# The head of a conditional residual kernel: adapter rows loaded ahead of the ids, adapters in falling order, and the work of the head in another order on every engine

## The chip, the cores and the metric

One core of a Trainium2 chip runs the kernel. The metric is the device time of one launch in microseconds (us), lower is better. Engines: TensorE (PE) multiplies, VectorE (DVE), ScalarE (ACT) and GpSimd (POOL) work on elements, SyncE (SP) here only issues DMAs; ACT issues DMAs too.

## The reference, cut to what matters

```python
# x: (128, 64, 1024) f32; cond ids in 0..15, adapter ids in 3..7, one of each per sample
# L0 weights: (16, 64, 64); L1 weights: (8, 1024, 1024)
x = x + einsum('bct,bcd->bdt', x, L0_weights[cond_ids])
x = x + einsum('bsi,boi->bso', x, L1_weight[adapter_ids])
```

With a one added on the diagonal of both weights each step is a single product. The ids of these inputs give 19, 27, 23, 25 and 34 samples to adapters 3, 4, 5, 6 and 7.

## The kernel before

The 128 samples are sorted by adapter on the chip and dealt into slots of two samples with one adapter: 66 slots, of which the last of an adapter with an odd count holds one sample. For a slot PE first makes z = x times the adapter (1024 x 1024, in two halves n of 512 columns, KT = 8 row tiles), then y = z times the 64 x 64 condition weight. Products are kept exact by splitting every operand into a high part and the rest: `sum_z` does three products a tile (L557, L558, L560), and only two (no L560) where the slot holds one sample, whose rest then stands in the rows of the missing sample. `sum_y` (L570) is four products. PE's order of work in slot s: first half of z of s, y of slot s - 1, second half of z of s. The last slot has an order of its own (`sum_last_z`, L638 to L641, in pieces of 512, 256 and 256 columns, `sum_last_y`, L652), with DVE and ACT taking y out of the banks (L786, L1086) and stores by SP (L498, three, or two with one sample) and ACT (L810, one, none with one sample).

Who does what for a slot: SP loads x of slot s + 2 (eight DMAs, L442) and one chunk of 128 rows of the next adapter (four DMAs, L459), if there is one to load: the first eight slots after the first of each adapter load one each. POOL adds the one to the chunk (L305) and makes the low part of x (`xt_lo`, L353) and of the chunk (L370). DVE turns the chunk (L975), makes the low part of z's first half (L998), finishes y of the slot before (L1005), turns x of slot s + 2 (L990), and makes the low part of z's second half (L998), in that order. ACT makes the high parts (L699, L704, L695), spreads the condition weights (L709), moves y (L715) and stores y (L263). Every engine runs its own list in order and waits on semaphores.

The head, before the first product (L557), is straight code:

- SP loads the adapter ids as one row, the condition weights (w0, L400), waits for `first_known`, reads the smallest adapter id and loads its first two chunks (L409), waits for `samples_made`, loads x of slot 0 (L420) and the other six chunks; chunks 6 and 7 go into the places of chunks 0 and 1 and wait until those are turned. Then the table of slots is moved into one row (L424), and x of slots 1 and 2 is loaded from `table_i` (L442). Then it waits for the last turning and for `table_ready` (L1048), and the loop of slots begins.
- ACT loads both kinds of ids once more, one to a partition (L675, L676).
- DVE clips the ids in a row (L852 to L859) and in a column (L862 to L870), builds `member` (L871), finds the two samples of slot 0 (to L887), and from the counts of members (`counted`, PE L524 and L525) ranks the samples (L890 to L918, `hot_made`); PE gathers by rank (L599, L600), and DVE makes the table (L923 to L947, `table_made`). `link` makes each op wait for the one before.
- For each chunk POOL adds the one (L312), PE turns it (`turn_first`, eight transposes, L538) into a pair of banks of which there are three, ACT copies the high part (L687) and DVE makes the low part (L831) in two halves n. x of slot 0 is turned in the same row of steps (`TURN_ORDER`); the last chunk's turning stands behind the first nine products. A turning waits until the low part three steps before is made.
- w0 gets its one from POOL (L339), its high part from ACT (L750), its low part from POOL (L345).

## Time and profile before

| what | us |
|---|---|
| median of 3 runs | 795.91 |
| range of these runs | 795.88 to 796.24 |
| the profiled execution | 799.4 |
| its span, first to last instruction | 797.7 |
| busy in the span: PE, DVE, ACT, POOL | 780.7, 590.1, 455.9, 254.5 |

The page of the profile gives busy time by engine, the chain of work that ended last, and the costliest groups of instructions. The trace behind it can be asked for the instructions of one stretch in order of time, for waits, and for busy time by stretch. Times in the rows are microseconds from the start of the span, unless a column says otherwise.

### The profile page before, as it was taken

How to read it: one execution, taken by the hardware profiler on the slowest of the kernel's cores; microseconds unless marked ns; L12 is line 12 of the kernel's file. 1: busy time of each engine (PE TensorE's matmuls, PEld its weight loads, DVE VectorE, ACT ScalarE, POOL GpSimd, SP SyncE). 2: the span in 40 equal slices, each digit the busy share in tenths (PEclk: the TensorE clock that was granted, in tenths of full speed). 3: DMA queues.
4: the chain of work that ended last, by engine and by line, in shares of the span. 5: the costliest groups of instructions: out<-in, count | busy, mean ns of one | idle time of the engine just before them, and what ended most of it. 6: DMA issues, size and time to landing. Idle time of an engine off the chain costs nothing.

```text
span 797.7 us, 19299 instructions
## 1 busy us (share of the span) xinstructions
PE 780.7 (98%) x3480; PEld 646.8 (81%) x3481; DVE 590.1 (74%) x707; ACT 455.9 (57%) x773; POOL 254.5 (32%) x158
## 2 busy tenths in 40 slices
PE   5999999999999999999999999999999999999997
PEld 4788888888888888888888888888888888888885
DVE  7777987788887567888876788887576756756764
ACT  3565666566556555765655566566554654555554
POOL 1444434243452212335431243452122122122110
PEclk9999999999999999999999999999999999999998
DMA  8345454444532334444333444532332233233133
GB/s 249 98 110 153 128 144 122 124 123 138 154 99 85 105 91 119 128 148 139 98 105 105 121 121 141 156 97 88 105 96 76 78 105 91 67 105 102 60 102 81
DMA packets 73956, 90.91 MB, mean 114 GB/s; under 512 B 13781, under 2 KB 64470, under 8 KB 73942
## 3 DMA queue, kind: packets, MB, share of 16 engines
q1 hardware_dynamic: 63654, 58.11, 24.2%
q10 hardware_dynamic: 10288, 32.65, 14.4%
q8 instruction: 5, 0.08, 0.0%
q14 instruction: 9, 0.07, 0.0%
HBM read 57.15 MB, written 33.55 MB: 114 GB/s over the span
## 4 chain that ended last, share of the span: by engine, by line
PE 97%; DMA 2%; DVE 0%; POOL 0%; issue 0%; SPq 0%; ACT 0%; POOLq 0%
PE z_ps L557 15%; PE z_ps L558 15%; PE first_ps L557 15%; PE first_ps L558 15%; PE z_ps L560 15%; PE first_ps L560 13%; PE y_ps L570 7%; DMA w_nat<-in_L_cond_weight_dram 2%; PE y_ps L538 0%; PE first_ps L538 0%; PE first_ps L641 0%; PE first_ps L639 0%; PE first_ps L638 0%; PE y_ps L652 0%; POOL w_nat L312 0%
## 5 line engine op out<-in xcount | busy, mean ns | idle before, releaser
L353 POOL TENSOR_TENSOR xt_lo<-x_turned,xt_hi 128x1024 fp32r<-128x1024 f32 x61 | 146.6, 2403 | 250.5 <-ACT xt_hi L699 246.5
L557 PE MATMUL z_ps<-w_hi,xt_hi 128*128 (+1 forms) x528 | 205.8, 390 | 0.0
L558 PE MATMUL z_ps<-w_lo,xt_hi 128*128 (+1 forms) x528 | 205.4, 389 | 0.0
L557 PE MATMUL first_ps<-w_hi,xt_hi 128*128 x520 | 202.4, 389 | 0.0
L558 PE MATMUL first_ps<-w_lo,xt_hi 128*128 x520 | 202.3, 389 | 0.0
L560 PE MATMUL z_ps<-w_hi,xt_lo 128*128 (+1 forms) x512 | 199.2, 389 | 0.0
L1005 DVE TENSOR_TENSOR y<-y_ps,y 64x512 f32<-64x512 f32 x252 | 173.2, 689 | 31.9 <-ACT y L715 26.0
L560 PE MATMUL first_ps<-w_hi,xt_lo 128*128 x472 | 183.6, 389 | 0.0
L715 ACT ACTIVATE y<-y_ps 64x512 f32<-64x512 f32 x252 | 149.1, 593 | 9.9 <-issue 2.0
L704 ACT ACTIVATE z_parts<-z_ps 64x512 fp32r<-64x512 f32 x132 | 78.4, 594 | 130.2 <-PE y_ps L570 92.8
L704 ACT ACTIVATE z_parts<-first_ps 64x512 fp32r<-64x512 f32 x130 | 77.2, 594 | 129.4 <-PE y_ps L570 102.8
L998 DVE TENSOR_TENSOR z_parts<-first_ps,z_parts 64x512 fp32r<-64x512 f32 x130 | 89.5, 689 | 76.2 <-ACT z_parts L704 72.9
L990 DVE STREAM_TRANSPOSE x_turned<-x_in 128x1024 f32<-128x1024 f32 x66 | 142.3, 2156 | 1.9
L998 DVE TENSOR_TENSOR z_parts<-z_ps,z_parts 64x512 fp32r<-64x512 f32 x132 | 90.9, 689 | 70.3 <-ACT z_parts L704 67.0
L370 POOL TENSOR_TENSOR w_lo<-w_turned,w_hi x32 | 77.3, 2416 | 192.7 <-ACT w_hi L695 192.7
L557 PEld LDWEIGHTS z_ps<-w_hi,xt_hi 128*128 128x128 f32 x528 | 99.1, 188 | 20.9 <-issue 0.5
L558 PEld LDWEIGHTS z_ps<-w_lo,xt_hi 128*128 128x128 f32 x528 | 99.1, 188 | 20.4
L557 PEld LDWEIGHTS first_ps<-w_hi,xt_hi 128*128 128x128 f32 x520 | 97.6, 188 | 20.6 <-issue 0.3
L558 PEld LDWEIGHTS first_ps<-w_lo,xt_hi 128*128 128x128 f32 x520 | 97.6, 188 | 20.2
L560 PEld LDWEIGHTS z_ps<-w_hi,xt_lo 128*128 128x128 f32 x512 | 96.1, 188 | 20.0
L560 PEld LDWEIGHTS first_ps<-w_hi,xt_lo 128*128 128x128 f32 x472 | 88.6, 188 | 18.4
L699 ACT ACTIVATE xt_hi<-x_turned 128x1024 fp32r<-128x1024 f32 x66 | 70.1, 1062 | 42.1 <-DVE x_turned L990 41.9
(147 smaller groups left out, 387.6 us busy)
## 6 DMA issues: line engine op xcount, KB each, us to landing
x_in<-in_x_dram SPq DMA_DIRECT2D x536, 64.0 KB, 2.6
...
w_nat<-in_L_cond_weight_dram SPq DMA_DIRECT2D x128, 128.0 KB
...
```

The costliest lines, as they stand in the source:

```text
L353: nc.gpsimd.tensor_tensor(xt_lo[h][:], x_turned[h][:], xt_hi[h][:].bitcast(F32), ALU.subtract).then_inc(xt_lo_made, 1)
L370: nc.gpsimd.tensor_tensor(of_chunk(w_lo, k), turned(k), of_chunk(w_hi, k).bitcast(F32), ALU.subtract).then_inc(chunk_lo_made, 1)
L557: nc.tensor.matmul(to, xt_hi[h][:, t, :], whi, start=(t == 0), stop=False)
L558: mm = nc.tensor.matmul(to, xt_hi[h][:, t, :], wlo, start=False, stop=last and not pair)
L560: mm = nc.tensor.matmul(to, xt_lo[h][:, t, :], whi, start=False, stop=last)
L570: mm = nc.tensor.matmul(y_ps[n][k if pair else 0][:], w0_parts[:, k], z_parts[:, n, k], start=pair or k == 0, stop=pair or k == 1)
L699: nc.scalar.activation(xt_hi[h][:], x_turned[h][:], ACT.Copy).then_inc(xt_hi_made, 1)
L704: nc.scalar.activation(z_parts[rows_of(k), n, k], z_banks[h][n][rows_of(k)], ACT.Copy).then_inc(z_hi_made, 1)
L715: nc.scalar.activation(y[h][rows_of(k), n * HALF:(n + 1) * HALF], y_ps[n][k][rows_of(1 - k)], ACT.Copy).then_inc(y_begun, 1 if pair else 2)
L990: nc.vector.transpose(x_turned[h][:].rearrange("p t (b m) -> p b t m", m=BLOCK), x_in[h][:].rearrange("p (b m t) -> p b t m", b=BLOCKS, m= ...
L998: nc.vector.tensor_tensor(z_parts[rows_of(1 - k), n, k], z_banks[h][n][rows_of(k)], z_parts[rows_of(k), n, k].bitcast(F32), ALU.subtract). ...
L1005: nc.vector.tensor_tensor(own, y_ps[n][k][rows_of(k)], own, ALU.add).then_inc(y_made, 1 if pair else 2)
```

## The change

- The adapter ids are replaced by 7 - id on the way in, and 7 - id again where an adapter is looked up, so the adapters are worked in falling order, 7 first.
- SP issues the first five chunks of adapter 7 right behind the row of ids, without knowing them. When the first adapter turns out to be another one they are loaded again; else SP only adds to their semaphores. w0 is loaded behind all chunks.
- The condition ids come as a row too, DVE clips them there, and PE spreads both rows over the partitions with two products. ACT's two loads of one id a partition are gone. PE begins with eight transposes of `ident` whose result nobody reads.
- x of slot 0 is turned sixth, not third; the gather stands behind four turnings, not one; the first products wait for six low parts, not five. Whether slot 0 holds one sample or two is known from the row chain (`first_samples_i[:, 2:3]`), not from the table.
- On DVE the halves of the low parts stand between the small ops of the ranking and the table; `turn_x` of slot 1 and the wait for w0's low part stand ahead of the two ops that make `table_ready`.
- x of slot 1 is loaded half by SP and half by ACT, ahead of ACT's last high part. SP loads the first chunk of the next adapter ahead of its look at the number of pairs.
- POOL adds the one to w0 ahead of its small ops on groups, and makes w0's low part without waiting for the table.
- ACT copies z's high part ahead of that of x of slot 1. In the last slot the wait for the stores of y stands later.

The diff, cut to its core:

```diff
         X0 = "x of slot 0"
-        TURN_ORDER = [0, 1, X0, 2, 3, 4, 5, 6, 7]
+        TURN_ORDER = [0, 1, 2, 3, 4, X0, 5, 6, 7]
         TURN_OF = {what: i for i, what in enumerate(TURN_ORDER)}
-        FOR_FIRST_HALF = 5
+        FOR_FIRST_HALF = 6
+        WARMING = 8
...
+        def load_sample(eng, sample, half, h):
+            for a in range(BLOCKS):
+                to = x_in[h][a * BLOCK:(a + 1) * BLOCK, half * HALF:(half + 1) * HALF]
+                eng.dma_start(to.rearrange("r (b m) -> r b m", m=QUARTER),
+                              x_quarters[bass.ds(sample, 1), a].rearrange("n r b m -> (n r) b m")
+                              ).then_inc(x_loaded[h], 16)
+
+        def look_early(eng, s, field):
+
+            return eng.value_load(table_i[s:s + 1, field:field + 1], min_val=0, max_val=TOP[field])
...
 
-                pool.wait_ge(first_loaded[c], 16)
+                pool.wait_ge(first_loaded[c], 32 if c < AHEAD_OF_IDS else 16)
                 nat = first_nat[c][:, c * P:(c + 1) * P]
...
+            pool.wait_ge(w0_loaded, 2 * 16)
+            nc.gpsimd.tensor_tensor(w0_nat, w0_nat,
+                                    two_ident[:].rearrange("p (n d) -> p n d", n=1).to_broadcast([P, NCOND, C]),
+                                    ALU.add).then_inc(w0_with_1, 1)
...
-            nc.gpsimd.tensor_copy(group_row[:], group_id[:]).then_inc(groups_ready, 1)
-
-            pool.wait_ge(w0_loaded, 2 * 16)
-            nc.gpsimd.tensor_tensor(w0_nat, w0_nat,
-                                    two_ident[:].rearrange("p (n d) -> p n d", n=1).to_broadcast([P, NCOND, C]),
-                                    ALU.add).then_inc(w0_with_1, 1)
+            nc.gpsimd.tensor_scalar(group_row[:], group_id[:], -1.0, float(NAD - 1), ALU.mult, ALU.add).then_inc(groups_ready, 1)
+
             pool.wait_ge(w0_hi_made, 1)
-
-            pool.wait_ge(table_ready, 1)
             nc.gpsimd.tensor_tensor(w0_all[:, :, 1], w0_nat, w0_all[:, :, 0].bitcast(F32),
...
+            for c in range(AHEAD_OF_IDS):
+                sp.dma_start(first_nat[c], adapter_rows[((NAD - 1) * CHUNKS_PER_GROUP + c) * P:((NAD - 1) * CHUNKS_PER_GROUP + c + 1) * P, :]).then_inc(first_loaded[c], 16)
+
+            sp.wait_ge(first_known, 1)
+            first_ad = sp.value_load(first_row[0:1, 0:1], min_val=0, max_val=NAD - 1)
...
+            with sp.If(first_ad < NAD - 1):
+                for c in range(AHEAD_OF_IDS):
+                    sp.wait_ge(first_loaded[c], 16)
+                    load_first(c)
+            with sp.Else():
+
+                for c in range(AHEAD_OF_IDS):
+                    sp.sem_inc(first_loaded[c], 16)
+
+            sp.wait_ge(samples_made, 2)
+            _, first_samples = nc.values_load_multi_w_load_instructions(
+                first_samples_i[0:1, 0:2], engines=[sp.engine], min_val=0, max_val=B - 1,
+                skip_runtime_bounds_check_because="the table is made on the chip, of clipped indices")
+            for k, sample in enumerate(first_samples):
+                sp.dma_start(x_in[0][k * C:(k + 1) * C, :], x_rows[bass.ds(sample * C, C), :]).then_inc(x0_loaded, 16)
+            for c in range(AHEAD_OF_IDS, CHUNKS_PER_GROUP):
+                if c >= OWN_PLACE:
+                    sp.wait_ge(first_turned, NH * TURN_OF[c - OWN_PLACE] + NH)
+                load_first(c)
             with nc.allow_non_contiguous_dma(reason="rows of one condition"):
                 for lo in (0, C):
                     sp.dma_start(w0_nat[lo:lo + C], cond_rows).then_inc(w0_loaded, 16)
-
-            sp.wait_ge(first_known, 1)
-            first_ad = sp.value_load(first_row[0:1, 0:1], min_val=0, max_val=NAD - 1)
-
-            def load_first(c):
-                if c >= OWN_PLACE:
...
-            for c in range(2):
-                load_first(c)
-
-            sp.wait_ge(samples_made, 1)
...
-            for c in range(2, CHUNKS_PER_GROUP):
-                load_first(c)
-            sp.wait_ge(table_made, 1)
-            sp.dma_start(slot_row[:, 1:LOOKED_UP + 1, :], table_i[0:LOOKED_UP]).then_inc(table_moved, 16)
...
-            load_early_x(1, 1)
+
+            sp.wait_ge(table_made, 1)
+            load_sample(sp, look_early(sp, 1, SAMPLE_A), 0, 1)
+            sp.dma_start(slot_row[:, 1:LOOKED_UP + 1, :], table_i[0:LOOKED_UP]).then_inc(table_moved, 16)
             sp.sem_inc(x_loaded[0], PER_X)
 
             sp.wait_ge(first_turned, NH * TURN_OF[X0] + NH)
-            load_early_x(2, 0)
-
-            sp.wait_ge(table_moved, 16)
+            load_samples([look_early(sp, 2, field) for field in (SAMPLE_A, SAMPLE_B)], 0)
+
+            sp.wait_ge(first_turned, NH * len(TURN_ORDER))
+            sp.wait_ge(groups_ready, 1)
+            sp.wait_ge(table_ready, 1)
+            up_to, = look(sp, 1, CHUNKS)
+            load_chunks_between(0, up_to)
             pairs_past = look_pairs_past(sp)
-            sp.wait_ge(table_ready, 1)
-            sp.wait_ge(groups_ready, 1)
-            sp.wait_ge(first_turned, NH * len(TURN_ORDER))
-            load_chunks(0)
...
+            for _ in range(WARMING):
+                nc.tensor.transpose(first_banks[2][0][:, 0:P], ident[:], ident[:])
+            pe.wait_ge(row_clipped, 1)
+            nc.tensor.matmul(ids_ps[:, 0:1], clipped_row, ones[0:1, 0:1], start=True, stop=True)
+            pe.wait_ge(row_clipped, 2)
+            nc.tensor.matmul(ids_ps[:, 1:2], cond_row, ones[0:1, 0:1], start=True, stop=True).then_inc(ids_spread, 1)
...
-            turn_first(0)
+            for i in range(TURNS + 1):
+                turn_first(i)
...
-            for i in range(1, len(TURN_ORDER) - LAST_TURNS):
+            for i in range(TURNS + 1, len(TURN_ORDER) - LAST_TURNS):
                 turn_first(i)
 
-            pe.wait_ge(table_made, 1)
+            pe.wait_ge(samples_made, 2)
...
+            act.dma_start(cond_row_i, cond_ids.rearrange("(u b) -> u b", u=1)).then_inc(cond_row_loaded, 16)
...
-            for i in range(len(TURN_ORDER)):
+            for i in range(len(TURN_ORDER) - 1):
                 keep_first_hi(i)
+
+            act.wait_ge(table_made, 1)
+            load_sample(act, look_early(act, 1, SAMPLE_B), 1, 1)
+            keep_first_hi(len(TURN_ORDER) - 1)
             act.wait_ge(w0_with_1, 1)
             nc.scalar.activation(w0_all[:, :, 0], w0_nat, ACT.Copy).then_inc(w0_hi_made, 1)
             act.sem_inc(xt_hi_made, 1)
+            keep_z_hi(0, 0, 0)
             keep_xt_hi(1, 1)
-            keep_z_hi(0, 0, 0)
             act.wait_ge(table_ready, 1)
...
-            act.wait_ge(y_stored[1], 32 * pairs_past + STORED_AHEAD)
...
                 with act.If(stores > 1):
+                    act.wait_ge(y_stored[1], 32 * pairs_past + STORED_AHEAD)
                     act.wait_ge(y_summed, PER_Y * s + 2 * part + 1)
...
-            row_link(nc.vector.tensor_copy(ids_row, ids_row_i))
+            row_link(nc.vector.tensor_scalar(ids_row, ids_row_i, -1.0, float(NAD - 1), ALU.mult, ALU.add))
             row_link(nc.vector.tensor_scalar(wrap_row, ids_row_i, 0.0, float(NAD), ALU.is_lt, ALU.mult))
             row_linked()
-            row_link(nc.vector.tensor_tensor(wrapped_row, ids_row, wrap_row, ALU.add))
+            row_link(nc.vector.tensor_tensor(wrapped_row, ids_row, wrap_row, ALU.subtract))
+            dve.wait_ge(cond_row_loaded, 16)
+            row_link(nc.vector.tensor_scalar(cond_wrap_row, cond_row_i, 0.0, float(NCOND), ALU.is_lt, ALU.mult))
             row_linked()
-            row_link(nc.vector.tensor_scalar(clipped_row, wrapped_row, 0.0, float(NAD - 1), ALU.max, ALU.min))
+            nc.vector.tensor_scalar(clipped_row, wrapped_row, 0.0, float(NAD - 1), ALU.max, ALU.min).then_inc(row_clipped, 1)
+            row_link(nc.vector.tensor_tensor(cond_wrapped_row, cond_row_i, cond_wrap_row, ALU.add))
+            dve.wait_ge(row_clipped, 1)
+            row_link(nc.vector.tensor_reduce(first_id[:], clipped_row, AX_X, ALU.min))
             row_linked()
-            row_link(nc.vector.tensor_reduce(first_id[:], clipped_row, AX_X, ALU.min))
-            dve.wait_ge(ids_loaded, 32)
-            for f, n in ((0, NAD), (1, NCOND)):
...
+            dve.wait_ge(ids_spread, 1)
+            link(nc.vector.tensor_copy(ids[:], ids_ps))
             link(nc.vector.tensor_scalar(member[:], col[:, 0:NAD], ids[:, 0:1], None, ALU.is_equal))
...
+            nc.vector.tensor_scalar(first_samples_i[:, 2:3], second_place[:], 0.0, 1.0, ALU.is_lt, ALU.add
+                                    ).then_inc(samples_made, 1)
...
+            sum_before(0, cnt)
+            keep_first_lo(0, (0,))
+            stepped()
+            sum_before(1, sums[0])
+            keep_first_lo(0, (1,))
+            stepped()
+            sum_before(2, sums[1])
+            keep_first_lo(1, (0,))
+            stepped()
+            total = sums[2]
+            step(nc.vector.tensor_tensor(looked[:, 1:3, :], total[:], cnt[:], ALU.subtract))
+            keep_first_lo(1, (1,))
+            stepped()
+            step(nc.vector.tensor_scalar(pair_count[:, 0:1], total[0:1, 0, NAD - 1:NAD], -1.0, None, ALU.add))
             link(nc.vector.tensor_tensor(picked[:], looked[:],
                                          member[:].rearrange("p (u a) -> p u a", u=1).to_broadcast([P, 3, NAD]),
                                          ALU.mult))
-            link(nc.vector.tensor_reduce(own[:], picked[:], AX_X, ALU.add))
-            link(nc.vector.scalar_tensor_tensor(out=pos[:], in0=own[:, 1:2], scalar=2.0, in1=own[:, 0:1],
+            step(nc.vector.tensor_scalar(pair_count[:, 1:2], pair_count[:, 0:1], 1, None, ALU.logical_shift_right))
+            step(nc.vector.tensor_reduce(own[:], picked[:], AX_X, ALU.add))
+            keep_first_lo(2, (0,))
+            stepped()
+            step(nc.vector.scalar_tensor_tensor(out=pos[:], in0=own[:, 1:2], scalar=2.0, in1=own[:, 0:1],
                                                 op0=ALU.mult, op1=ALU.add))
             nc.vector.tensor_copy(vals[:, 0:1], row[:])
             nc.vector.tensor_copy(vals[:, 1:2], ids[:, 1:2])
             nc.vector.tensor_copy(vals[:, 2:4], own[:, 1:3])
             nc.vector.memset(vals[:, 4:5], 1.0)
...
+            keep_first_lo(2, (1,))
+            keep_first_lo(3)
...
+            keep_first_lo(4, (1,))
+            keep_x0_lo(TURN_OF[X0])
+            stepped()
+            step(nc.vector.tensor_scalar(fill[:], got[:, 0, 0:2], absent[:, 0:1], None, ALU.mult))
+            link(nc.vector.tensor_scalar(rank[:, 1:2], rank[:, 0:1], float(CHUNKS_PER_GROUP), None, ALU.min))
...
-            for i in range(1, TURN_OF[X0]):
-                keep_first_lo(i)
-            keep_x0_lo(TURN_OF[X0])
             for i in range(TURN_OF[X0] + 1, len(TURN_ORDER)):
                 keep_first_lo(i)
             dve.wait_ge(first_lo_made, NH * len(TURN_ORDER))
             dve.sem_inc(x_is_turned, 1)
             dve.sem_inc(xt_lo_made, 1)
             dve.sem_inc(chunk_lo_made, CHUNKS_PER_GROUP)
+            turn_x(0, 1)
+
```

## Rows read from the trace of the kernel before

**Rows 1.** The chain that ended last, by engine (page, part 4).
```profile
PE 97%; DMA 2%; DVE 0%; POOL 0%; issue 0%; SPq 0%; ACT 0%; POOLq 0%
```

**Rows 2.** Busy time: stretch, length, engines (count), granted clock, DMA share, GB/s.
```profile
0.00:25.00 25.00, 13.93 (x73) 12.19 (x75) 18.62 (x82) 9.92 (x18) 4.78 (x19) 1.00 0.82 237
...
100.00:400.00 300.00, 300.00 (x1325) 248.15 (x1324) 237.03 (x250) 180.02 (x300) 112.53 (x63) 1.00 0.41 122
```

**Rows 3.** The chain in order of time, to 30 us: start, us, what.
```profile
11.74 11.54 DMA w_nat<-in_L_cond_weight_dram
```

**Rows 4.** The head in order of time: start, us, engine, line, operation, idle before.
```profile
7.12 0.15 DVE L890 TENSOR_SCALAR cnt<-z_ps 128x8 f32<-128x8 f32 x1
...
9.59 1.97 PE L538 MATMUL first_ps<-ident,w_nat 128*128 128x128 f32 x8 [2.80 <-POOL w_nat L312]
...
10.43 0.28 DVE L918 TENSOR_SCALAR x_turned<-x_turned,pos 128x128 f32<-128x128 f32 x1
...
15.04 0.17 DVE L947 CAST table_i<-table 128x9 int32<-128x9 f32 x1
...
18.77 1.16 PE L538 MATMUL y_ps<-ident,w_turned 128*128 128x128 f32 x8
...
24.88 0.49 PE L557 MATMUL z_ps<-w_hi,xt_hi 128*128 128x512 f32 x1
...
28.31 1.29 DVE L831 TENSOR_TENSOR w_lo<-y_ps,w_hi 128x512 fp32r<-128x512 f32 x2 [1.78 <-ACT w_hi L687]
...
30.59 2.16 DVE L990 STREAM_TRANSPOSE x_turned<-x_in 128x1024 f32<-128x1024 f32 x1
...
33.92 2.40 POOL L353 TENSOR_TENSOR xt_lo<-x_turned,xt_hi 128x1024 fp32r<-128x1024 f32 x1 [0.69 <-ACT xt_hi L699]
```

**Rows 5.** The SP queue's DMA issues, 14 to 62 us, in order of time.
```profile
17.45 8.94 SPq L442 DMA_DIRECT2D x_in<-in_x_dram  x16
33.29 2.98 SPq L459 DMA_DIRECT2D w_nat<-in_L_cond_weight_dram  x4
37.51 4.87 SPq L442 DMA_DIRECT2D x_in<-in_x_dram  x8
```

**Rows 6.** Waits of the SP queue, 33 to 130 us: total, times, longest.
```profile
SPq L459 <- DVE w_turned L975: 0.3, 2, 0.2
```

**Rows 7.** The x loads to 60 us: issue in ns, minimum, median, maximum, and landing.
```profile
L442 SPq DMA_DIRECT2D x_in<-in_x_dram x32: 316/317/1505, 17.4 to 53.9; - x32
...
DMA to landing us min/median/max: 2.0/3.0/6.0
```

**Rows 8.** DVE in order of time, slots 1 and 4.
```profile
42.57 2.17 DVE L975 STREAM_TRANSPOSE w_turned<-w_nat 128x1024 f32<-128x1024 f32 x1 [3.10 <-POOL w_nat L305]
...
51.30 1.41 DVE L998 TENSOR_TENSOR z_parts<-first_ps,z_parts 64x512 fp32r<-64x512 f32 x2
...
87.49 1.41 DVE L998 TENSOR_TENSOR z_parts<-z_ps,z_parts 64x512 fp32r<-64x512 f32 x2
```

**Rows 9.** The chain in order of time: PE's y groups of slots 1 and 4.
```profile
54.22 0.91 PE y_ps L570 x4
...
89.58 0.91 PE y_ps L570 x4
```

**Rows 10.** The same view: y groups two apart, a slot of one sample between.
```profile
286.40 0.91 PE y_ps L570 x4
...
306.35 0.93 PE y_ps L570 x4
```

**Rows 11.** The tail: DVE in time, the chain's middle y group, landings of L498, L810.
```profile
788.26 1.41 DVE L1005 TENSOR_TENSOR y<-y_ps,y 64x512 f32<-64x512 f32 x2
...
790.03 0.47 PE y_ps L652 x4
...
DMA to landing us min/median/max: 2.6/2.6/2.8
...
DMA to landing us min/median/max: 4.0/4.0/4.0
```

179 lines of the change are left out of this document (82 added, 97 removed).

## The prediction, made before the changed kernel was run

> **What bounds the kernel now.** I read the chain of waits first. TensorE (PE) holds 97% of it [rows 1], and by the busy time of stretches PE is never idle between 25 us and the tail, while of the first 25 us it is busy for 13.93 [rows 2]. So only three things can move the end: when the first product starts, what opens a gap behind it, and the tail. The chain in order of time shows the head: the load of adapter rows issued at 11.74 us holds it for 11.54 us [rows 3], and the first product starts at 24.88 [rows 4].
>
> Then I ask how much room the other engines have once PE runs, since a head that ends earlier meets them where they stand. The SP queue is the one to look at. From its chunk load at 33.29 us on it issues without a pause: x follows at 37.51, right behind the four chunk loads [rows 5], and in the 97 us after 33 the largest entry of its waits is 0.3 us for two [rows 6]. It runs at its own pace there, not at PE's. Behind each chunk come POOL and VectorE (DVE): the chunk is turned, z_lo, y, the turning of x, the second z_lo. For slot 1 that second z_lo ends at 51.30 + 1.41 = 52.71, and PE's y group begins at 54.22; for slot 4 it ends at 88.90 and the group begins at 89.58 [rows 8, 9]. The k = 1 part is read by the fourth matmul of that group, 3 x 0.227 later (0.91 for four), so the room is 54.90 - 52.71 = 2.2 us in slot 1 and 90.26 - 88.90 = 1.36 us in slot 4, the smallest of the first five. The PE groups are 11.79 apart (35.36 for three).
>
> **The change part by part.**
>
> *Loads ahead of the ids, falling order.* The ids mapped to 7 - id have adapter 7 as their smallest, and adapter 7 is in the data (34 of 128 samples), so the five early chunks are the right ones, and SP takes the branch that only adds to semaphores. They are issued from about 1.4 us, not from 5.65 (the w0 loads go behind). Bytes up to chunk 6 are 8 x 0.52 = 4.2 MB. At a mean of 300 GB/s (237 over the whole head, [rows 2]) from 2.7 us chunk 6 is in at 16 to 18 us. The DMAs leave the head's path.
>
> *Ids by PE.* Two K = 1 matmuls replace the scattered loads and some ops. The row chain gets 3 ops more and the column chain loses 4; I put member at 5.9 where it was 5.65, and the counts are used at 7.1 as before [rows 4], because the sample ops run until then. Nothing gained, 0 to 0.5 lost.
>
> *DVE becomes the head's path.* Before, the ops from the counts (7.12) to hot end at 10.71, the gather follows, and the table is cast at 15.04 [rows 4]. Now w_lo halves stand between them. A half costs 0.645 (1.29 for two, [rows 4]). Up to hot there are five: 3.6 us of ops, less some 0.8 of link gaps that they fill, plus 3.2, and up to 1.2 of waits for ScalarE (ACT): hot at 14.4. Three more halves reach 16.4; got, absent, rank and the table columns take 1.6 for 18.0 with one half among them; then one half and two of x of slot 0 give 20.1. The last table ops (six links of 0.2) cast the table at 21.3, where it was 15.2. The chunk of the seventh turning needs w_lo of item 4 (18.7) and takes 1.16. So the first product starts at 20.2, not 24.88: 4.7 us sooner (bounds 19 and 22.5: all waits hidden; all turnings at the slow pace).
>
> For the pace: eight turnings took 1.97 us at 9.59 and 1.16 at 18.77, the granted clock being shown as 1.00 (2.4 GHz) throughout [rows 2, 4]; PE had turned almost without pause in between. I count on the quick ones from 11 to 13 us, PE being at work from 7 on. The Trainium skill (TensorE: Matmul & The Clock Gate, Part 4) says that transposes do not count as PE activity, which speaks against the eight warming ones; this trace disagrees, as PE did nothing but transposes before it sped up. By the page the turnings would stay slow and the first product start near 22.
>
> *x of slot 1 by SP and ACT.* It hangs on the table, so it starts at 22.3. ACT issues four at 0.6 (4.87 for eight, [rows 5]), which pushes its last w_hi to 24.6; the last w_lo ends at 26.4 and PE needs it at 26.65 (24 products and a turning behind 20.2): nothing. x lands 3.0 us behind its issue in the median [rows 7], so at 27.3 to 28.5. From the start of turn_x to that of xt_lo it is 3.3 us, and xt_lo takes 2.4 [rows 4]: 33.1 to 34.3. PE took slot 1 at 36.98 (54.22 less half a slot's 24 products and a slot) and would now want it at 32.3. So 1 to 2 of the 4.7 us go here; 2.6 to 3.8 are left. The w0 chain (add, copy and subtract, of xt_lo's and xt_hi's size, 2.4 + 1.1 + 2.4), now ahead of the two slot_row ops on DVE, ends by 29, beside turn_x, so the table row is ready near 29.9 (30.55 before): covered; if w0 landed after 22 it would show one for one.
>
> *Where the SP queue ends up.* Before, x of slots 1 and 2 was issued from 17.45, and the queue then stood waiting for the last turning and the table row until 30.55. Now it begins at 21.3 + 1.0: four x loads 2.0, the slot_row DMA 1.0, two value loads 1.6, eight x loads 4.4, so 31.3. A shorter way through the looks (2.0 where 2.7 passed) puts chunk 0 at 33.3. That is where it was: the old wait is replaced by issue time. Moving look_pairs_past behind chunk 0 (0.6) makes x of slot 3 and chunk 1 0.6 later than 37.51 and 44.91. Bounds for the later loads: 1 us earlier (short value loads) and 2.5 us later (table 1.5 late and a stalled issue; single x issues took up to 1.5 us [rows 7]).
>
> So PE arrives 2.6 to 3.8 us early and the z_lo it wants comes 0.6 us later than before. Room 1.36 - 0.6 = 0.8 us: that is what stays after slot 4. The rest becomes waits of PE before y groups in slots 2 to 5. What is late next would be xt_lo of the slots, with 2.6 us of room, so it doesn't show.
>
> *The falling order at the other end.* The data have 19, 27, 23, 25 and 34 samples for adapters 3 to 7: 66 slots either way, four of them with one sample. Before, all four lie in the middle, each worth 2 x 11.79 - 19.95 = 3.63 us [rows 9, 10]. Now the one of adapter 3 is the last slot. Its first half still saves 8 x 0.227 = 1.81. Its second half saves 16 x 0.12 of PE time, but its middle y group waits for DVE, whose ops there stand one behind the other up to 789.67 whatever PE does; PE was at that group at 790.03 [rows 11], so 0.3 is left. At the end no DVE copy and no ACT store are needed; SP stores half as much. SP's stores landed in 2.6 us, ACT's last in 4.0 [rows 11]: 1.3 saved, or nothing if the lone store takes 4. Sum: -3.63 + 1.81 + 0.3 + 1.3 = 0.2 us lost, 1.6 at worst. The wait on y_stored that moved in ACT costs nothing: its store landed at the time at which w_parts would be 2 us sooner, and take_last_y comes 4 us behind.
>
> **Sum.** Profiled execution: 799.4 us, span 797.7, 3.5 above the median of 795.91; I take differences over. -0.8 + 0.2 = -0.6: span 797.1, median 795.3.
>
> **The rivals.**
> A. *The head carries through.* If SP's early loop isn't what its lack of waits suggests (issue gets quicker once fewer DMAs are in flight, or the table is ready a us or two sooner), PE keeps about 3. For: single issues vary between 0.3 and 1.5 us [rows 7]. Against: DVE waited 3.1 us for the first chunk, which came in 6 us behind its last issue [rows 5, 8], and SP has no wait that could shrink. Time: 795.9 - 3.0 + 0.2 = 793.1.
> B. *SP later than the room.* The table waits behind eleven halves on DVE, and everything SP issues from there waits behind it. Each us beyond 22.0 for table_i shifts all chunk loads, and from 1.36 us of shift on PE ends later than before. At table_i = 24 (ACT or PE feeding the halves late): 3.3 - 1.36 = 1.9, plus 0.2: 798.0. Turnings that stay at the slow pace (chance 0.06) are the mild form: four on the path at 0.8 more each, of which DVE's ops cover half, so 1.65 us: 0.6 + 1.65 - 1.36 = 0.9, plus 0.2: 797.0, at the forecast's upper end and counted there. (The skill's rule on transposes, above, would bring that about.) For B: DVE had 18.6 us of work in the 25 [rows 2]. Against: its ops are known, and with all waits of my estimate doubled the cast is at 22.5.
> C. *The early loads do not do what they say*, the head still ending with chunk 6 at 23 because the five loads, x and chunk 5 share the engines: 795.9 + 0.2 + 0, and 1.6 at worst. It gives a time inside the forecast's, so only its place differs.
>
> **How the numbers follow.** Forecast 0.50 (794.6 to 797.0), A 0.28, B 0.14, C 0.08. What a measurement can tell from no change is 0.2%, 1.6 us: faster than 794.3 or slower than 797.5. Faster: A, and 0.03 of the forecast, 0.31. Slower: B, and 0.02 of C, 0.16. Same: 0.53. The range takes in A's middle and stops short of B's: 792.9 to 797.5.
>
> **What would show each step.** First product near 20.2, table cast near 21.3, chunk 6 long in before its add: the head. Chunk 0's issue near 33.3 and the next x near 38.1; PE waits for z_parts in y groups of slots 2 to 5 adding up to 2 to 3 us; y groups 11.79 apart from then on. The last slot without matmuls of L641 and with 1.5 us of PE waiting before its middle y group. I am wrong if chunk 0 is issued before 32 or after 35, if PE shows no gap between 35 and 100 us, or if the last store lands more than 3 us behind its issue.

## The result and the profile after

The changed kernel takes 797.7 us in the median (797.3 to 798.7), the kernel before 795.91 (795.4 to 797.8): ratio 1.0021, 95% interval 1.0013 to 1.0029. It is 1.8 us slower. The forecast was 795.3, within 792.9 to 797.5.

The profiled execution of the changed kernel takes 798.37 us, its span is 796.7. First the chain that ended last by engine (the page), and the busy time of stretches (columns as in [rows 2]).

```profile
PE 92%; DVE 2%; issue 2%; SPq 1%; DMA 1%; ACTq 1%; ACT 0%; DVEq 0%; POOL 0%; POOLq 0%
...
0.00:25.00 25.00, 21.02 (x116) 19.09 (x118) 20.14 (x86) 12.23 (x22) 9.19 (x28) 1.00 0.76 232
```

PE is busy for 21.02 of the first 25 us, not 13.93 [rows 2], yet its share of the chain has fallen from 97% [rows 1] to 92%: the head was won, and the chain leaves PE elsewhere. The head in order of time, lines of three engines (columns as in [rows 4]; the line at 16.91 is POOL's add on chunk 6, that at 20.56 its add on w0):

```profile
13.34 0.27 DVE L983 TENSOR_SCALAR x_turned<-x_turned,pos 128x128 f32<-128x128 f32 x1
...
16.91 0.45 POOL L330 TENSOR_TENSOR w_nat<-w_nat,ident 128x128 f32<-128x128 f32 x1 [1.14 <-DMA w_nat<-in_L_cond_weight_dram]
...
18.53 0.50 PE L576 MATMUL z_ps<-w_hi,xt_hi 128*128 128x512 f32 x1
...
19.51 0.17 DVE L1015 CAST table_i<-table 128x9 int32<-128x9 f32 x1
...
20.56 2.39 POOL L340 TENSOR_TENSOR w_turned<-w_turned,two_ident 128x1024 f32<-128x1024 f32 x1 [1.76 <-DMA w_turned<-in_L_cond_weights_dram]
```

The first product starts at 18.53 instead of 24.88 [rows 4]. Now where the chain leaves PE, slots 0 to 2 (start, us, what):

```profile
33.88 7.10 DMA w_nat<-in_L_cond_weight_dram
41.22 0.46 POOL w_nat L323
...
48.30 2.15 DVE x_turned L1041
50.49 0.50 DVE z_parts L1049
51.20 0.70 DVE z_parts L1049
52.04 0.47 PE y_ps L589
...
63.82 0.91 PE y_ps L589 x4
```

PE's y groups of slots 0 to 2 end at 38.62, 52.51 and 64.72. Before, slot 1 ended at 54.22 + 0.91 = 55.13 [rows 9], and its neighbours 11.79 to each side. So of the 6.35 us 4.7 are left at slot 0, 2.6 at slot 1 and 2.2 at slot 2, from where on the groups are 11.79 apart. They went into waits of PE (those of 0.8 us and more behind the first product: us in total, times, longest; then one smaller wait, from PE's order of time):

```profile
PE y_ps L672 <- DVE y L1056: 1.7, 1, 1.7
PE z_ps L672 <- ACT w_parts L727: 1.4, 1, 1.4
PE first_ps L576 <- POOL xt_lo L369: 1.3, 1, 1.3
PE y_ps L672 <- DVE z_parts L1125: 1.0, 1, 1.0
PE y_ps L589 <- DVE z_parts L1049: 0.8, 2, 0.5
...
44.50 0.49 PE L576 MATMUL z_ps<-w_hi,xt_hi 128*128 x1 [0.44 <-POOL xt_lo L369]
```

The third is slot 1's wait for xt_lo, the fifth the two waits for z_parts, both inside the y group of slot 1, at 51.2 and 52.0. The first, second and fourth are in the tail. The line at 44.50 is a wait for xt_lo of slot 2, which POOL makes behind its add on chunk 0. And SP's queue, the counterpart of [rows 5] (SPq and ACTq lines are DMA issues of SP and ScalarE):

```profile
20.45 1.94 SPq L289 DMA_DIRECT2D x_in<-in_x_dram  x4
22.43 0.97 SPq L487 DMA_DIRECT2D slot_row<-table_i  x1
25.70 3.84 SPq L289 DMA_DIRECT2D x_in<-in_x_dram  x8
31.43 3.01 SPq L469 DMA_DIRECT2D w_nat<-in_L_cond_weight_dram  x4
36.30 3.83 SPq L289 DMA_DIRECT2D x_in<-in_x_dram  x8
```

There is a puzzle in this. Span against span the changed kernel is 1.0 us *shorter* (796.7 and 797.7), by the timed executions it is 1.8 longer. One of the two profiles can't be typical, and 799.4 us, the execution profiled before, lies above all eleven timed ones.

### The profile page after: what moved, and what is told of

The parts are those of the page before. It is cut to its first block, busy times and chain, and to the rows that moved or that the text cites. A ratio compares the mean times of both kernels' runs of the same rounds, so it can differ in the third digit from the quotient of the medians.

```text
span 796.7 us, 19304 instructions
## 1 busy us (share of the span) xinstructions
PE 782.7 (98%) x3484; PEld 648.1 (81%) x3485; DVE 589.1 (74%) x705; ACT 455.8 (57%) x775; POOL 254.0 (32%) x158
## 4 chain that ended last, share of the span: by engine, by line
PE 92%; DVE 2%; issue 2%; SPq 1%; DMA 1%; ACTq 1%; ACT 0%; DVEq 0%; POOL 0%; POOLq 0%
PE z_ps L576 14%; PE z_ps L577 14%; PE z_ps L579 14%; PE first_ps L577 14%; PE first_ps L576 14%; PE first_ps L579 13%; PE y_ps L589 7%; DMA w_nat<-in_L_cond_weight_dram 1%; SPq L289 1%; DVE x_turned L1041 1%; DVE w_lo L862 0%; ACTq L231 0%; DVE y L1056 0%; SPq L469 0%; PE y_ps L537 0%
## 5 line engine op out<-in xcount | busy, mean ns | idle before, releaser
L579 PE MATMUL z_ps<-w_hi,xt_lo 128*128 (+1 forms) x528 | 205.7, 390 | 0.0
L1056 DVE TENSOR_TENSOR y<-y_ps,y 64x512 f32<-64x512 f32 x254 | 174.6, 688 | 28.2 <-ACT y L733 22.2
L579 PE MATMUL first_ps<-w_hi,xt_lo 128*128 x464 | 180.7, 389 | 0.0
L576 PEld LDWEIGHTS z_ps<-w_hi,xt_hi 128*128 128x128 f32 x528 | 99.1, 188 | 22.2 <-issue 1.6
L579 PEld LDWEIGHTS z_ps<-w_hi,xt_lo 128*128 128x128 f32 x528 | 99.2, 188 | 20.6
L577 PEld LDWEIGHTS first_ps<-w_lo,xt_hi 128*128 128x128 f32 x520 | 97.7, 188 | 20.2
```

Source lines behind the costliest of these rows:

```text
L576: nc.tensor.matmul(to, xt_hi[h][:, t, :], whi, start=(t == 0), stop=False)
L577: mm = nc.tensor.matmul(to, xt_hi[h][:, t, :], wlo, start=False, stop=last and not pair)
L579: mm = nc.tensor.matmul(to, xt_lo[h][:, t, :], whi, start=False, stop=last)
L1056: nc.vector.tensor_tensor(own, y_ps[n][k][rows_of(k)], own, ALU.add).then_inc(y_made, 1 if pair else 2)
```

## The experiments

Every kernel below has one edit in common: where an engine waits for a count that follows from a table value, it waits for max(count, 1), in eight places (the expectations say seven). before_again and after_again are the two kernels with this edit alone. Ratios are to the kernel before, timed on the same chip, with 95% intervals. "head_only" is the changed kernel with rising order; the edits are shown against the kernel that each names.

**The two kernels once more: is the profile of before typical?**

> The kernel before, but in seven places where an engine waits for a count that follows from a table value, the count is first made max(count, 1). All my kernels carry this; here it is measured alone: 795.9 us, within 0.3 of before, if it costs nothing. The profile is the second purpose. Theory 1 (the profiled execution of before had a head some 3.5 us longer than its timed executions, so that my differences were taken from a wrong starting point): this one has a span of 794 to 796, the first product before 24, and y groups of slots 0 and 1 ending near 40 and 52 instead of 43.34 and 55.13. Rival: a profile always lengthens the head of this kernel, then the span is 797.7 and the first product is at 24.9 again.

> The changed kernel with the same seven max operations: 797.7 us, span of the profile 796.7, first product near 18.5, y groups of slots 0 to 3 ending near 38.6, 52.5, 64.7, 76.5. If the head of the profiled executions varies, these move by over 1 us; else within 0.3.

before_again: 795.87, ratio 0.9998 (0.9988 to 1.0007); after_again: 797.77, 1.0016 (1.0007 to 1.0025). The max operations cost nothing that shows. before_again's span is 794.4, 3.3 less than in the first profile. Its head, by the chain, then SP's queue and POOL:

```profile
11.86 7.92 DMA w_nat<-in_L_cond_weight_dram
...
31.05 2.98 SPq L464 DMA_DIRECT2D w_nat<-in_L_cond_weight_dram  x4
...
39.59 0.46 POOL L310 TENSOR_TENSOR w_nat<-w_nat,ident 128x128 f32 x1 [6.59 <-DMA w_nat<-in_L_cond_weight_dram]
...
62.64 0.92 PE y_ps L575 x4
```

The load that held the head took 7.92 us where it took 11.54 [rows 3]; the first product starts at 21.55, slot 2's y group ends at 63.55, and PE doesn't wait between 22 and 120 us. Theory 1 holds, and four more profiles of the old head (before_x2, order_only, order_looks and order_both, below) agree: their first products start at 21.4 to 22.2. Chunk 0 is issued at 31.05, not 33.29 [rows 5], since POOL's w0 add (24.04 here, 27.25 there) and the table row behind it had been late in the first profile too. In after_again the first product starts at 18.57 as before, but slot 1 waits 2.0 for xt_lo and then runs at half pace (last section); slot 2 ends at 64.86. So a typical head of before is ahead of the changed one at slot 2: 63.55 (63.6 to 64.3 in the other four) against 64.7 to 64.9.

**The two halves of the change alone.** order_only, against before (the first id and the ids of the column are mapped the same way):

```
-row_link(nc.vector.tensor_copy(ids_row, ids_row_i))
+row_link(nc.vector.tensor_scalar(ids_row, ids_row_i, -1.0, float(NAD - 1), ALU.mult, ALU.add))
...
-nc.gpsimd.tensor_copy(group_row[:], group_id[:])...
+nc.gpsimd.tensor_scalar(group_row[:], group_id[:], -1.0, float(NAD - 1), ALU.mult, ALU.add)...
```

head_only, against the changed kernel:

```
-adapter_rows[((NAD - 1) * CHUNKS_PER_GROUP + c) * P: ...]
+adapter_rows[(EARLY * CHUNKS_PER_GROUP + c) * P: ...]        (EARLY = 3)
-with sp.If(first_ad < NAD - 1):
+with sp.If(first_ad < EARLY):
...
(and the four maps to NAD - 1 - x taken out)
```

> The kernel before with the falling order of adapters alone (ids and group rows mapped to 7 - id; loads, spreading and x queues as before). Theory 2 (the order costs what the tail cannot give back: 3.63 lost in the middle, some 2.0 saved at the end, because ScalarE's sequencer reads its looks behind the store issues and holds the last slot's first z copy at 3.4 us behind the store): 1.6 us above before_again, 797.5. The prediction's step: 0.2 above, 796.1. In the profile the last slot shows the one sample, and the z copy comes 3.4 us behind the store issue of the slot before.

> The changed kernel with rising order: the five early loads take rows of adapter 3, the smallest one in this data, as a constant. Theory 2 with theory 1 (the new head brings almost nothing against the timed executions, since after slot 1 PE waits for chunk work of the SP queue): 0 to 0.4 us above before_again, 796 to 796.3, although the first product is some 5 us earlier. The prediction's step: 0.8 below, 795.1. A head that costs the whole 1.8 (the order costing 0.2) would give 797.5.

order_only: 798.3, 1.0024 (1.0014 to 1.0035). head_only: 796.53, 1.0001 (0.9990 to 1.0013). The order costs 1.9 us where 0.2 was forecast, the head brings nothing where 0.8 was forecast, and the two make up the whole loss. Both terms of the sum are wrong, in the same direction. What follows takes them one at a time.

**The head: is it the SP queue?** In the chain above PE's y group of slot 1 ends 52.51 - 41.22 = 11.3 us behind the start of chunk 0's add. That distance, and when chunk 0 was issued, can be compared over profiles (first product; first DMA of chunk 0; start of its add on POOL; ends of the y groups of slots 1 and 2; all from the order of time, * where PE waited for z_parts at slot 1):

```
kernel           product  issue   add    slot 1   slot 2
before            24.88   33.29  41.98   55.13    66.91
before_again      21.55   31.05  39.59   51.76    63.55
after             18.53   31.43  41.21   52.51 *  64.72
head_only         19.03   32.01  40.74   52.13 *  64.30
act_chunk0        20.81   31.83  42.75   54.10 *  66.31
act_looks         19.13   31.72  40.63   51.99 *  64.14
no_warming        18.55   31.57  40.15   51.50 *  63.67
x2_split_again    19.84   30.77  40.68   52.01 *  64.17
falling_again     18.62   29.69  38.03   50.41    62.20
x1_by_sp          18.57   33.83  42.09   53.61    65.59
```

In all six rows with * slot 1 ends 11.30 to 11.39 behind the add and slot 2 another 12.15 to 12.21 behind that. So I take it that slot 2 doesn't end before add + 23.5, and no row does. In before that is 65.5, 1.4 ahead of 66.91: the room that the prediction measured (1.36). In before_again it is 63.1 against 63.55: the room is 0.45.

Four edits to the SP queue. act_chunk0 (against head_only) has ScalarE issue chunk 0's four DMAs; one_look has SP read the two samples of slot 2 in one load; x1_by_sp undoes the split of x of slot 1; x2_split splits x of slot 2 as well:

```
 act_chunk0, ScalarE behind place_w0(0):
...                                (its waits and its look for the number of chunks)
+with act.If(any_chunk > 0):
+    for b in range(BLOCKS):
+        act.dma_start(w_nat[:, 0, b * QUARTER:(b + 1) * QUARTER], ...).then_inc(chunk_loaded[0], 16)
 one_look, SP:
-load_samples([look_early(sp, 2, field) for field in (SAMPLE_A, SAMPLE_B)], 0)
+_, samples = nc.values_load_multi_w_load_instructions(table_i[2:3, SAMPLE_A:SAMPLE_B + 1], engines=[sp.engine], ...)
+load_samples(samples, 0)
 x1_by_sp:
+load_sample(sp, look_early(sp, 1, SAMPLE_B), 1, 1)
-load_sample(act, look_early(act, 1, SAMPLE_B), 1, 1)
 x2_split:
-load_samples([look_early(sp, 2, field) for field in (SAMPLE_A, SAMPLE_B)], 0)
+load_sample(sp, look_early(sp, 2, SAMPLE_A), 0, 0)
+load_sample(act, look_early(act, 2, SAMPLE_B), 1, 0)          (behind its copy of w0)
```

> head_only (the changed kernel with rising order) with the four DMAs of chunk 0 issued by ScalarE behind place_w0(0), near 29.9 us, instead of by the SP queue behind x of slot 2, near 32.0. The SP queue is free 3.4 us earlier for x of slot 3, chunk 1 and all that follows. Theory 3 (the new head gains nothing because PE waits at the y groups of slots 1 and 2 for work behind chunk 0, which hangs on the SP queue): those waits (1.3 and 0.4 in head_only) go, the y group of slot 2 ends near 62.6 instead of 64.3, and the time is 1.5 us below head_only: 794.8. Rival 3b (the waits stand for something else, xt_lo of slot 1 or DVE's own load): the y group of slot 2 ends at 64.3 as before, 796.3.

> head_only with the two samples of slot 2 read by one load of two values on SP, as in the kernel before, instead of two value loads one after the other with an assertion each (24.05 to 26.09 us there). SP's x of slot 2 and chunk 0 come 1.2 us earlier. Theory 3: the y group of slot 2 ends 0.8 to 1.2 sooner than in head_only (64.3), the time is 0.8 to 1.2 below it: 795.3. Rival 3b: no change, 796.3.

act_chunk0: 796.39, 0.9999 (0.9990 to 1.0007), the rival's number. But the edit did not remove the cause. ScalarE's queue, POOL's add, SP's queue:

```profile
31.83 3.69 ACTq L791 DMA_DIRECT2D w_nat<-in_L_cond_weight_dram  x4
...
42.75 0.46 POOL L329 TENSOR_TENSOR w_nat<-w_nat,ident 128x128 f32 x1 [8.95 <-DMA w_nat<-in_L_cond_weight_dram]
...
29.91 8.96 SPq L295 DMA_DIRECT2D x_in<-in_x_dram  x11
```

ScalarE came to it at 31.83, took 3.69 us for what takes SP 3.0, and SP's x of slot 3 went out at the same time; the chunk landed 2 us later than in head_only, and slots 1 and 2 followed it by 11.35 and 12.21. It settles nothing on the time and is one more row for the distance. one_look: 795.23, 0.9992 (0.9983 to 1.0001), the number of theory 3, but within its error of no effect; in its profile chunk 0 goes out at 31.59, only 0.4 earlier, and slot 2 ends at 64.94, not 0.8 to 1.2 sooner than 64.3 (the clock, last section), so it is no proof.

> head_only with all eight DMAs of x of slot 1 issued by SP (one part of the change undone). In every profile so far the y group of slot 1 ends 11.6 us behind chunk 0's landing (the start of its add on POOL) when PE waits for it, and that landing is some 9 us behind chunk 0's first issue. Theory 3 (after the first product the SP queue sets the pace): SP's x of slot 2 and chunk 0 come 2.5 us later than in head_only (34.5 instead of 32.0), the y group of slot 2 ends near 66.5 instead of 64.3, and the time is 1.5 to 2.2 above head_only, near 798.3. Rival 3b (it is x of slot 1 and xt_lo alone): x of slot 1 lands 1.5 later, half of it shows, and the time is 0.7 above head_only: 797.1.

> head_only with x of slot 2 split as the change splits x of slot 1: the first sample by SP with one look, the second by ScalarE behind its copy of w0. SP is free 3 us earlier, then held by the table row (28.2 in head_only): chunk 0 goes out near 29.5 instead of 32.0. Theory 3: the waits at the y groups of slots 1 and 2 go; what is left is the wait for xt_lo of slot 1; the y group of slot 2 ends near 62.6 to 63, and the time is 1.2 to 1.7 below head_only: 794.9. Rival 3b: no change, 796.4. Rival 3c (chunk 0's landing doesn't follow its issue, because other loads are then under way beside it, as in act_chunk0, where it landed 7.5 us behind the last issue): its add starts at 40 again and nothing is won.

x1_by_sp: 798.42, 1.0033 (1.0022 to 1.0043), forecast 798.3 by theory 3 and 797.1 by the rival. x2_split: 794.8, 0.9984 (0.9975 to 0.9993), forecast 794.9 and 796.4. By the ratios one sample's loads more on SP cost 2.5 us against head_only, and one less wins 1.4. In x1_by_sp PE loses 1.8 more between slots 2 and 5 (slot 5 ends at 102.78, 37.19 behind slot 2 and not 3 x 11.79 = 35.37): the later chunks don't catch up there, and PE waits for z_parts in the y group of slot 4. Up to slot 2 the profile doesn't part theory 3 from rival 3b: slot 0 already ends at 41.82, 2.8 later than in head_only (a wait of 2.9 us for xt_lo, and the clock behind it, last section), and from there alone slot 2 would end at 65.4 of the 65.59. What speaks for the SP queue here is the loss behind slot 2 and the size of the whole. x2_split's SP queue and POOL's add, the waits of its SP queue, and POOL's add in the second profile of the same kernel (x2_split_again):

```profile
25.14 1.85 SPq L295 DMA_DIRECT2D x_in<-in_x_dram  x4
30.01 2.99 SPq L475 DMA_DIRECT2D w_nat<-in_L_cond_weight_dram  x4
...
38.09 0.46 POOL L329 TENSOR_TENSOR w_nat<-w_nat,ident 128x128 f32 x1 [6.13 <-DMA w_nat<-in_L_cond_weight_dram]
...
SPq L501 <- DVE slot_row L1106: 1.1, 1, 1.1
...
40.68 0.46 POOL L329 TENSOR_TENSOR w_nat<-w_nat,ident 128x128 f32 x1 [7.94 <-DMA w_nat<-in_L_cond_weight_dram]
```

In x2_split chunk 0 is issued 2.0 us earlier than in head_only and PE waits at no y group of slots 1 and 2, but slot 2 still ends at 64.12, because of the clock (last section). In x2_split_again chunk 0 is issued 1.2 earlier than in head_only (30.77), yet its add starts where it did (40.68 and 40.74), PE waits at slot 1 again, and slot 2 ends at 64.17, against 64.30: that is rival 3c, in one execution. Only falling_again's profile, with the same edit, shows the whole path (29.69, 38.03, 62.20). So the gain stands on the times, measured twice; that it comes by chunk 0 is shown in one profile out of three, and the intervals of x2_split (0.9975 to 0.9993) and head_only (0.9990 to 1.0013) just touch. The line of the waits of SP says what is late next: the table row.

**What else stands in the head.** w0_early has the two w0 loads ahead of chunks 5 to 7; table_early (against x2_split) has DVE's ops on the table row ahead of the turning of x of slot 1 and not behind POOL's w0 subtract; no_warming is the changed kernel with WARMING = 0; before_x2 splits x of slot 2 in the kernel before.

> head_only with the two w0 loads issued ahead of chunks 5 to 7 instead of behind them. POOL's queue after the chunks is: w0 add (begins 20.2 to 22.4 in seven profiles, at the landing of w0), group ops, w0 subtract, looks, xt_lo of slot 1 (begins 29.3 to 31.4, some 8.8 us behind), and PE waits 1.3 to 2.0 for that. With w0 there at 18 the add follows chunk 7's add at once, near 19.8. Theory 4 (that POOL chain, not the landing of x of slot 1, sets PE's wait at slot 1): xt_lo begins near 28.7 and PE's wait falls to under 1.0; the time changes by less than 0.5, since the y group of slot 1 waits for chunk 0 anyway. If chunks 6 and 7 come later by the 1 MB ahead of them, the first product comes 0.5 to 1.5 later, also at no cost in the end: 796.4.

w0_early: 797.05, 1.0010 (1.0001 to 1.0019). The chunks behind w0 came late: the last two adds of POOL start at 19.96 and 21.19 (16.91 and 18.35 in the changed kernel), the first product at 22.39, and the w0 add at 21.60, no earlier than before. Half of the expectation fell (xt_lo was no earlier), the other half stood: the first product is 3.4 us later than in head_only, the time by its ratio only 0.7.

> x2_split with DVE's two ops on the table row ahead of the turning of x of slot 1, and no longer behind POOL's w0 subtract. The table row is ready near 25.7 instead of 28.1. SP, which waited for it from 27.0 to 28.2 in x2_split, issues chunk 0 near 28.8 instead of 30.0, POOL's looks for xt_lo come 0.7 us earlier. Theory 3: PE's wait for xt_lo of slot 1 falls from 1.3 to 1.8 to about 0.7, its products behind it keep the quick pace, the y group of slot 2 ends near 62, and the time is 0.3 to 1.0 below x2_split: 794.2, ratio 0.9978. Rival: DVE and POOL have other work that holds xt_lo, then nothing changes and it stays at 794.8.

table_early: 796.13, 0.9996 (0.9986 to 1.0006). A miss: chunk 0 went out at 29.77 instead of 30.01, xt_lo of slot 1 began at 31.06, later than in x2_split (29.58), and PE waited 2.5 for it. The trace shows why: the first of DVE's two ops on the row started 2.1 us earlier (25.32, not 27.46), but beside POOL's w0 subtract, and took 2.20 us:

```profile
24.98 2.38 POOL L367 TENSOR_TENSOR w_all<-w_turned,w_all 128x1024 fp32r<-128x1024 f32 x1
...
25.32 2.20 DVE L1099 TENSOR_TENSOR slot_row<-slot_row 1x69 int32<-1x69 int32 x1 [0.53 <-DMA slot_row<-table_i]
```

Where no such POOL op runs beside it, in sixteen profiles, the op takes 0.21 to 0.29. Here it ended 0.16 behind the subtract (last section), so the row was ready at 27.8 instead of 28.1, and the turning of x of slot 1 had been put behind it. What an earlier row is worth was therefore not measured.

> The changed kernel without the eight transposes at the start (WARMING = 0). If transposes do warm the clock, the turnings of the first chunks stay at 1.9 to 2.0 us for longer than until 12 us, hot and the table come later by under 1 us, and the first product starts 0 to 1 us later. If they don't, nothing in the head moves by more than 0.2. By theory 3 the time is 797.7 either way, since the first product's start has room; by the prediction's account it would go up by what the head loses, up to 798.7.

no_warming: 798.85 in five executions, 1.0036 (1.0023 to 1.0049), against 1.0016 (1.0007 to 1.0025) and 1.0021 (1.0013 to 1.0029) for the changed kernel. In its profile (span 795.6, 797.27 us, the fastest of the five) nothing in the head is later: hot at 13.34, the first product at 18.55, slot 2 at 63.67. So the eight transposes move nothing that the profile shows; the timed difference of 0.15 to 0.2%, whose intervals just overlap, has no place in it, and stays open.

> The kernel before with x of slot 2 split between SP and ScalarE. In its second profile PE has no gap between the first product (21.55) and the tail, so the y group of slot 2 ends 42.0 behind the first product. Theory 3: the old head hangs on the DMAs of its adapter chunks and not on the SP queue; earlier chunk loads win nothing, 1.0000, within 0.4 us. Rival: the SP queue bounds the timed executions of the old head too, and 1 us is won, 0.9987.

before_x2: 795.48, 0.9995 (0.9986 to 1.0004). Chunk 0 is issued 1.2 us earlier (29.87) and slot 2 ends where it did (63.58, first product 21.42 + 42.16). In the old head PE has no wait behind its first product that an earlier chunk 0 could shorten; what holds it is the adapter load ahead of the first product (11.86 in before_again, above), where the new head's PE waits for chunk 0. The two ends happen to lie about 1 us apart.

**The order: what doesn't the tail give back?** The counterparts of the tail: ScalarE's DMAs and operations from the last stores of the loop on, in after, order_only and before_again.

```profile
781.16 1.13 ACTq L270 DMA_DIRECT2D out_dram<-y  x2
784.62 1.21 ACT L722 ACTIVATE z_parts<-first_ps 64x512 fp32r<-64x512 f32 x2 [3.50 <-issue]
```

```profile
780.81 1.13 ACTq L268 DMA_DIRECT2D out_dram<-y  x2
784.26 1.21 ACT L709 ACTIVATE z_parts<-first_ps 64x512 fp32r<-64x512 f32 x2 [3.48 <-issue]
```

```profile
780.25 1.21 ACT L709 ACTIVATE z_parts<-first_ps 64x512 fp32r<-64x512 f32 x2 [3.49 <-PE y_ps L575]
```

With a full last slot (before_again) this first z copy waits for PE, whose y group ends at 780.44. With a one-sample last slot PE is there 1.82 earlier (9.97 behind the y group before it, not 11.79), and ScalarE's sequencer isn't: "issue" is a wait for nothing that the profile shows. Between the stores and the copy it reads two rows of the table into its registers (a look) for the last slot. The chain of after shows the first:

```profile
782.81 1.19 ACTq L231
```

The second follows at 784.13 and takes 0.29. act_looks (the changed kernel) and order_looks (order_only) have these two looks ahead of the loop:

```
+before, s = 2 * pairs_past, 2 * pairs_past + 1
+_, sample, stores = look(act, s, SAMPLE_A, STORES)
+stores_before, = look(act, before, STORES)
 with act.Fori(0, pairs_past) as i:
     ...
-(the same three lines)
```

> The changed kernel with ScalarE's two looks for the last slot (sample and number of stores, and those of the slot before) taken ahead of its loop instead of behind the store DMAs of the last pass. Nothing else moves. Theory 2 (the order loses 1.6 to 1.9 because ScalarE's sequencer holds the last slot's first z copy 3.4 us behind the store issue): the copy comes 1.4 to 1.9 us earlier, PE's wait of 1.4 for w_parts goes, and the span ends 1.2 to 1.9 us sooner, so 796.2 instead of 797.7. Rival 2b (DVE's ops in the tail stand one behind the other and set the end anyway, as the prediction's step said): within 0.4 of the changed kernel, 797.5.

> order_only with ScalarE's two looks for the last slot ahead of its loop. order_only was 1.0024 of before. From the y group of the last slot but one to the end of the span, the profiles show 25.8 us with a full last slot and rising order, 23.7 to 24.0 with the falling order, 22.2 with the falling order and the early looks; 3.63 less is what the one-sample slot takes from the middle and has to give back at the end. Theory 2 (the looks are the whole cost): 25.8 - 22.2 = 3.6, so the order is free, 1.0000, 795.9. Rival 2c (a cost of 1 us or more is left, of a kind that act_looks hid by a lucky head): 1.0013 or more, 797.

act_looks: 796.64, 1.0002 (0.9993 to 1.0011): against the 1.0016 and 1.0021 of the changed kernel 1.1 to 1.5 us are back. order_looks: 798.22, 1.0028 (1.0018 to 1.0039): nothing. ScalarE's rows of act_looks, then of order_looks:

```profile
780.87 1.13 ACTq L275 DMA_DIRECT2D out_dram<-y  x2
782.55 1.21 ACT L727 ACTIVATE z_parts<-first_ps 64x512 fp32r<-64x512 f32 x2 [1.71 <-PE y_ps L594]
783.85 0.51 ACT L732 ACTIVATE w_parts<-w_all 128x128 fp32r x2
```

```profile
780.34 1.13 ACTq L268 DMA_DIRECT2D out_dram<-y  x2
781.95 1.21 ACT L709 ACTIVATE z_parts<-first_ps 64x512 fp32r<-64x512 f32 x2 [1.64 <-PE y_ps L575]
784.88 0.75 ACT L714 ACTIVATE w_parts<-w_all 128x128 fp32r x2 [1.73 <-DMA out_dram<-y]
```

In both the z copy is early and waits for PE again. In order_looks w_parts then waits for a store to land: the wait on y_stored[1], which the change moved and order_looks did not. Two delays had covered each other. order_both moves that wait too:

```
-act.wait_ge(y_stored[1], 32 * pairs_past + STORED_AHEAD)     (ahead of place_w0(s))
 ...
+act.wait_ge(y_stored[1], 32 * pairs_past + STORED_AHEAD)     (in both branches of take_last_y)
```

> order_looks with the change's other edit of the tail as well: ScalarE's wait for the store of the slot before moved from ahead of place_w0 into take_last_y. Theory 2e (looks and store wait cover each other: each alone wins nothing, both together free the last slot's first z group): PE's wait of 1.2 for w_parts goes, from the last y group to the end of the span it is 12.1 to 12.2 us as in act_looks instead of 13.7, and the time is 1.5 below order_looks: ratio 1.000 to 1.001 of before, 796.2. Rival 2c (something else in the falling order costs 1 us or more): 1.002 or more.

order_both: 796.54, 0.9997 (0.9986 to 1.0008):

```profile
782.33 1.21 ACT L709 ACTIVATE z_parts<-first_ps 64x512 fp32r<-64x512 f32 x2 [1.64 <-PE y_ps L575]
783.69 0.77 ACT L714 ACTIVATE w_parts<-w_all 128x128 fp32r x2
```

PE's wait for w_parts is gone, and by the time the falling order costs nothing that the interval (1.1 us below to 0.6 above) lets one see. The trace gives less: from the last y group of L575 to the end of the span it is 12.8, between the 12.1 expected and the 13.7 of order_looks, so in that execution 0.7 of the cost is left. act_looks, with 12.2, shows it all back.

**Both together, and the best version.** falling_best is act_looks with x2_split's edit; it and x2_split were run twice.

> The changed kernel with ScalarE's two looks ahead of its loop (act_looks) and x of slot 2 split (x2_split). act_looks was 1.4 below the changed kernel, at 1.0002 of before. Theories 2 and 3: a further 1.2 to 1.7 from the head, 795.0, ratio 0.998 to 0.9985. If x2_split's idea fails: 796.4.

> x2_split once more: 0.9984 of before if the first reading was undisturbed (794.7); by a rival that the two readings of the split are the same effect of 0.8 us, 0.999.

> falling_best once more, on the chip of x2_split_again. Theories 2 and 3 (the order is free with the early looks, and the split wins 1.3): 0.9985 as x2_split. If it is 1.0000 again while x2_split is 0.9984, there is a cost in the falling order that neither theory names.

falling_best: 796.22, 1.0000 (0.9991 to 1.0009), a miss, then, as falling_again, 795.58, 0.9994 (0.9985 to 1.0003). x2_split_again: 794.9, 0.9987 (0.9975 to 0.9998). So the head with x of slot 2 split and the rising order is faster than both kernels, and than before by 1.0 to 1.3 us, in both of its readings. With the falling order 0.6 to 1.3 us of that doesn't show, about what the intervals allow; the profile of falling_again is the shortest of all (span 792.9, slot 2 at 62.20), so it isn't a cost that each execution has, and what it is stays open. The profile of falling_best is one of those with a late head:

```profile
19.39 1.48 PE L562 MATMUL y_ps<-ident,w_nat 128*128 128x128 f32 x8 [2.02 <-POOL w_nat L335]
```

PE waits 2.0 us for chunk 6 (its add starts at 18.89, in falling_again at 16.29), so the first product starts at 20.53, not 18.62, chunk 0 goes out at 31.80, not 29.69, and slot 2 ends at 64.35.

## Why the prediction was wrong, point by point

- *What bounds the kernel; the early loads; DVE as the head's path.* Right, and better than forecast: chunk 6 in at 16.9 (16 to 18), hot at 13.34 (14.4), the table cast at 19.51 (21.3), the first product at 18.53 (20.2). Rival C is out. But "the DMAs leave the head's path" holds only just: POOL waited 1.1 us for chunk 6 and PE 0.4 for POOL, where the prediction had it "long in before its add". Over the fourteen profiles of the new head that add starts at 16.2 to 18.9 (19.96 in w0_early), and in six of them PE waits 0.8 to 2.0 us for it.
- *The first failed step: "I take differences over".* The sum was made against an execution 3.5 us above the median, and the text said so, but took the head's lateness as a property of the kernel. It was the head that was late (the load of 11.54 us where before_again shows 7.92). Against before_again the first product is 3.0 us sooner, not 6.35.
- *x of slot 1.* Right in kind: 1.3 us of wait for xt_lo (1 to 2). In four profiles it cost 1.6 more by the clock, below. That xt_lo of the later slots "doesn't show" was off by a little: slot 2's cost 0.4, behind POOL's add on chunk 0.
- *Where the SP queue ends up: "that is where it was".* Chunk 0 was forecast at 33.3 and came at 31.43 (32.33 in after_again); an issue before 32 was one of the signs that the prediction set for being wrong. But "where it was" is 31.05 in before_again. The new head's chunk 0 is 0.4 to 1.3 later, not equal.
- *The room of 1.36.* The mechanism (SP's loop feeds DVE, PE waits at y groups, the rest of the gain goes there) is seen in the changed kernel's own chain, and the times of x1_by_sp and x2_split fit it in sign and size; their profiles show the place only in part. The term was mis-sized: the room was that of the late execution, and a typical one has 0.45. With chunk 0 later than that, the head's net is 0 by head_only instead of -0.8. The waits came at slot 1, not at 2 to 5 (0.8 us for z_parts and 0.4 for xt_lo; with the group taken apart by them they cost 2.5 us from slot 0 to slot 2, against the 2 to 3 forecast), because the first chunk lands last and the later ones catch up (from slot 2 on the y groups are 11.79 apart).
- *The falling order.* Forecast 0.2 lost, 1.6 at worst; measured 1.9 in order_only. The shorter first half (1.82 for 1.81) is right, and the end gives back at least what was forecast: from the last y product to the end it is 3.2 us where before_again has 5.0, 1.8 less for 1.3. The step that failed: that PE and DVE alone set the pace behind it. ScalarE was read by its operations, not by what its sequencer does between them, so the look behind the stores was invisible. From the last y group of L589 to the end the changed kernel takes 13.7 us, before_again 14.0; act_looks takes 12.2, which is 1.8 less than before_again, about the 1.6 that were forecast.
- *"The wait on y_stored that moved costs nothing".* True in the changed kernel only. Without the move, order_looks shows that it holds the same PE group 1.2 us once the looks are out of the way: the move is needed for the order to be free, and not enough.
- *The rivals.* The time of B came out (798.0), but not its mechanism: the table was not late (19.51), so that fit is luck. B's own sum doesn't hold together either: its 3.3 us for a table at 24 count from 21.3, where its sentence says "each us beyond 22.0". A needed an SP queue that could go quicker, and x2_split is that by an edit: it won 1.4 against head_only, half of A's amount.
